# Norm statistics taken by the stages ahead of two norms, and the first of these norms moved into the feed-forward stage, in a six-block decoder on one Trainium2 core

## What is computed

```
x = _layernorm(x + _L0_attn_ref(x, ...))
x = _layernorm(x + _L0_xattn_ref(ctx_2048, ctx_2048, x, ssm_kernel, D, 8))   # a long convolution
x = _layernorm(x + _L0_ffn_ref(x, weight, norm_weight))                      # a quantised linear layer
x = _layernorm(x + _L1_attn_ref(x, ...))                                     # the gated delta rule
x = _layernorm(x + _L1_xattn_ref(x, ctx_2048, ctx_2048, decay))
x = _layernorm(x + _L1_ffn_ref(x, W1, W2))

_layernorm(x): (x - mean) / sqrt(var + 1e-5), mean and var over the 512 features of a token

_L0_ffn_ref(x): xn = x / sqrt(mean(x * x) + 1e-6) * norm_weight
                scale = max(max(|xn|) over all tokens and features, 1e-5)
                xq = round(clip(xn / scale * 127)) / 127 * scale
                out = (xq @ ternary(weight).T) * w_scale
```

## Time and profile before

| | |
|---|---|
| device time, median of 3 runs | 3282.03 us (3278.84 to 3283.53) |
| the profiled execution: its own time, its span | 3278.3 us, 3276.6 us |
| busy over the span: PE, DVE, ACT, POOL | 2951.4, 2576.6, 2401.8, 1950.9 us |
| mean granted TensorE clock | 0.961 of full speed |

### The profile page before, as it was taken

One profiled execution on the slowest core, in us unless ns is written; L12 is line 12 of the kernel. 1 busy time (PEld: TensorE's weight loads), 2 busy tenths in 40 slices (PEclk: granted clock), 3 DMA queues, 4 the chain that ended last, 5 costly groups with the idle time before them and its releaser, 6 DMA issues. The chain is left out here.

```text
span 3276.6 us, 80440 instructions
## 1 busy us (share of the span) xinstructions
PE 2951.4 (90%) x29987; PEld 2015.7 (62%) x30006; DVE 2576.6 (79%) x4692; ACT 2401.8 (73%) x6066; POOL 1950.9 (60%) x2266
## 2 busy tenths in 40 slices
PE   7999887736899999999999999999999999997386
PEld 5666555514566666666676666766766667665243
DVE  4555568885788888888888888888888888886796
ACT  4444343435888888888888888888888888886554
POOL 1111166504877777788777787787877878774000
PEclk9999998968999999999999999999999999999699
DMA  5110043401010110101101011010110101100201
GB/s 219 40 33 27 20 146 108 139 10 58 21 34 21 47 34 23 38 21 47 34 21 40 21 46 34 21 41 21 40 41 21 41 21 36 45 21 1 103 1 52
DMA packets 63473, 146.50 MB, mean 45 GB/s; under 512 B 8704, under 2 KB 17536, under 8 KB 59904
## 3 DMA queue, kind: packets, MB, share of 16 engines
q1 hardware_dynamic: 63104, 141.53, 13.8%
HBM read 128.06 MB, written 13.45 MB: 43 GB/s over the span
## 5 line engine op out<-in xcount | busy, mean ns | idle before, releaser
L2153 DVE TENSOR_TENSOR delta_Pb<-delta_bank,delta_lev 128x512 f16<-128x512 f32 x448 | 310.4, 693 | 148.6 <-PE delta_bank L2482 148.6
L2145 DVE SCALAR_TENSOR_TENSOR delta_F<-delta_bank,delta_cw,delta_F 128x510 f32<-128x510 f32 (+1 forms) x512 | 381.5, 745 | 42.8 <-ACT delta_far L1955 28.7
L2456 PE MATMUL delta_bank<-delta_xh,delta_qkvh 128*128 128x512 f16 x1024 | 390.1, 381 | 6.9 <-DVE delta_F L2145 4.5
L2456 PE MATMUL delta_bank<-delta_xl,delta_qkvh 128*128 128x512 f16 x1024 | 389.2, 380 | 0.0
L2456 PE MATMUL delta_bank<-delta_xh,delta_qkvl 128*128 128x512 f16 x1024 | 388.7, 380 | 0.0
L1695 POOL TENSOR_TENSOR delta_F<-delta_F,delta_far 128x506 f32<-128x506 f32 x256 | 278.4, 1088 | 93.4 <-DVE delta_F L2145 93.4
L1675 POOL TENSOR_SCALAR_AFFINE_SELECT delta_LA<-delta_LA 128x512 f32<-128x512 f32 x128 | 81.5, 637 | 376.3 <-DVE delta_LA L2183 355.4
L2170 DVE CAST delta_XT<-delta_bank 128x512 f16<-128x512 f32 x384 | 262.8, 684 | 50.4 <-PE delta_bank L2501 47.3
L2441 PE MATMUL delta_bank<-delta_zh,delta_xh 128*128 128x256 f16 x1024 | 279.3, 273 | 0.6 <-ACT delta_gz L1977 0.6
L2441 PE MATMUL delta_bank<-delta_zh,delta_xl 128*128 128x256 f16 x1024 | 279.2, 273 | 0.0
L2441 PE MATMUL delta_bank<-delta_zl,delta_xh 128*128 128x256 f16 x1024 | 278.9, 272 | 0.0
(11 more groups left out here) (375 smaller groups left out, 10171.3 us busy)
## 6 DMA issues: line engine op xcount, KB each, us to landing
delta_Gb<-g_rows SPq DMA_DIRECT2D x64, 512.0 KB, 5.3
conv_wf<-in_W SPq DMA_DIRECT2D x72, 256.0 KB, 3.4
delta_st_qkv<-in_Wqkv SPq DMA_DIRECT2D x17, 1024.0 KB, 8.4
conv_T<-filters SPq DMA_DIRECT2D x32, 256.0 KB, 3.4
delta_st_zo<-in_Wz SPq DMA_DIRECT2D x16, 512.0 KB, 8.1
delta_st_zo<-in_Wout SPq DMA_DIRECT2D x16, 512.0 KB, 6.6
conv_ahead_C<-in_ctx_rev SPq DMA_DIRECT2D x1, 6144.0 KB, 27.7
ternary<-conv_spare SPq DMA_DIRECT2D x36, 128.0 KB, 2.8
```

The source lines that it names most:

```text
L2145: ve.scalar_tensor_tensor(dst, src, cw_tap(i, 3 - lag), dst, ALU.mult, ALU.add)\
L2153: ve.tensor_tensor(left(Pb[:, lvl, :, :], lvl), comp(bank[5], lvl), bc(lev[:, lvl, :].rearrange("p (n s) -> p n s", s=1 << lvl), 1, 8), AL ...
L2456: ins = te.matmul(bk[:, :], ww[:, QKV[job], kc, :], xx[:, kc, tok:tok + 512], start=(m == 0), stop=(m == 11))
```

## The change

1. `conv_stage` gets a tensor `mv` and takes the moments itself, behind its last additions: ScalarE for tiles 0 to 8 (`SUMMED_BY_ACT = 9`), each sum as soon as its tile has been added, then the nine squares; VectorE `bn_stats` and `bn_aggr` for tiles 9 to 15 behind its sixteenth addition. ScalarE's unused output goes to `zT`. The ScalarE table set is loaded here.
2. norm1 is no longer a stage. `ffn0_stage` makes rs, nb and `square` from the moments, ScalarE normalises all sixteen tiles, and VectorE scales tile i as soon as it is normalised.
3. The maximum of tile i-1 stands behind the scaling of tile i.
4. `ffn0_stage` takes the moments for norm2 as in 1: ScalarE sums tile i-5 behind its copy of tile i and takes nine squares behind the last copy; VectorE takes seven tiles behind its last addition. `norm_stage` with `moments` skips its own statistics and its table load.

```diff
+SUMMED_BY_ACT = 9
 conv_stage, ScalarE, behind its loop over heads:
+            nc.scalar.preload_act_table_set("natural_log_exp_and_others")
+            for i in range(SA):
+                act.wait_ge(za.sem, za.at(i + 1))
+                nc.scalar.activation(zT[:, :, i * P:(i + 1) * P], X[:, i, :].rearrange("p (a b) -> p a b", a=KC),
+                                     ACT.Identity, accum_out=sm[:, 0, i:i + 1]).then_inc(summed.sem, 1)
+            act.wait_ge(summed.sem, summed.at(SA))
+            nc.scalar.activation(sm[:, 1, :], sm[:, 0, :], ACT.Copy, scale=-1.0 / D).then_inc(squared.sem, 1)
+            act.wait_ge(squared.sem, squared.at(1))
+            for i in range(SA):
+                nc.scalar.activation(zT[:, :, i * P:(i + 1) * P], X[:, i, :].rearrange("p (a b) -> p a b", a=KC),
+                                     ACT.Square, bias=sm[:, 1, i:i + 1], accum_out=sm[:, 2, i:i + 1])\
+                    .then_inc(squared.sem, 1)
 conv_stage, VectorE, behind its additions:
+            for t in range(SA, NT):
+                dve.wait_ge(za.sem, za.at(t + 1))
+                ve.bn_stats(st[:, t - SA, :], X[:, t, :]).then_inc(stats.sem, 1)
+            for t in range(SA, NT):
+                ve.bn_aggr(mv[:, t, :], st[:, t - SA, :]).then_inc(mom.sem, 1)
+            dve.wait_ge(squared.sem, squared.at(SA + 1))
+            ve.tensor_scalar(mv[:, 0:SA, 0], sm[:, 1, :], -1.0, None, ALU.mult).then_inc(mom.sem, 1)
+            ve.tensor_scalar(mv[:, 0:SA, 1], sm[:, 2, :], 1.0 / D, None, ALU.mult).then_inc(mom.sem, 1)
 ffn0_stage, ScalarE:
-            s_.preload_act_table_set("natural_log_exp_and_others")
+            act.wait_ge(g["var"].sem, g["var"].at(1))
+            s_.activation(tn[:, :], var[:, :], ACT.Ln).then_inc(g["root"].sem, 1)
+            act.wait_ge(g["root"].sem, g["root"].at(1))
+            s_.activation(rs[:, :], tn[:, :], ACT.Exp, scale=-0.5).then_inc(g["root"].sem, 1)
             act.wait_ge(g["v"].sem, g["v"].at(1))
             ...
             s_.activation(r[:, :], t[:, :], ACT.Exp, scale=-0.5).then_inc(g["tab"].sem, 1)
+            act.wait_ge(g["shift"].sem, g["shift"].at(1))
+            for i in range(NT):
+                s_.activation(X[:, i, :], X[:, i, :], ACT.Identity, bias=nb[:, i:i + 1], scale=rs[:, i:i + 1])\
+                    .then_inc(g["normed"].sem, 1)
 ffn0_stage, ScalarE, in the loop over tiles behind the copy of tile i, and behind the loop:
+                if 0 <= i - 5 < SA:
+                    sum_of(i - 5)
+            means()
+            for i in range(SA):
+                squares_of(i)
 ffn0_stage, VectorE (ahead of this: var, the Newton step, nb, square):
-            for i in range(NT):
-                ve.scalar_tensor_tensor(xn[:, i, :], X[:, i, :], r[:, i:i + 1], gam[:, :], ALU.mult, ALU.mult)\
-                    .then_inc(g["xn"].sem, 1)
-            for i in range(NT):
+            def largest(i):
                 dve.wait_ge(g["xn"].sem, g["xn"].at(i + 1))
                 ve.tensor_reduce(mx[:, i:i + 1], xn[:, i, :], AX.X, ALU.max, apply_absolute_value=True)\
                     .then_inc(g["mx"].sem, 1)
+            for i in range(NT):
+                dve.wait_ge(g["normed"].sem, g["normed"].at(i + 1))
+                ve.scalar_tensor_tensor(xn[:, i, :], X[:, i, :], r[:, i:i + 1], gam[:, :], ALU.mult, ALU.mult)\
+                    .then_inc(g["xn"].sem, 1)
+                if i >= 1:
+                    largest(i - 1)
+            largest(NT - 1)
 decoder:
-            norm_stage(nc, X, "norm1", square=square)
-            ffn0_stage(nc, X, consts, ahead, a["gamma"], square)
-        norm_stage(nc, X, "norm2")
+                ffn0_stage(nc, X, consts, ahead, a["gamma"], mv1, mv2)
+            norm_stage(nc, X, "norm2", moments=mv2)
```

More of the change, by code:

```diff
@@ L105, with norm_stage @@
 STATS_BY_ACT = 5
-def norm_stage(nc, X, name, guarded=False, square=None, product=None):
+def norm_stage(nc, X, name, guarded=False, moments=None, product=None):
     with ExitStack() as ctx:
@@ L148, in _ @@
                     ve.tensor_scalar(X[:, i, :], X[:, i, :], iM[:, i:i + 1], None, ALU.mult).then_inc(sca.sem, 1)
-            for i in range(SA, NT):
+            for i in range(SA, NT if moments is None else SA):
                 if guarded:
@@ L152, in _ @@
                 ve.bn_stats(st[:, i, :], X[:, i, :]).then_inc(stats.sem, 1)
[L153 to L160 removed]
+            if moments is None:
+                for i in range(SA, NT):
+                    dve.wait_ge(stats.sem, stats.at(i + 1 - SA))
+                    ve.bn_aggr(mv[:, i, :], st[:, i, :]).then_inc(mom.sem, 1)
+                dve.wait_ge(squares.sem, squares.at(SA + 1))
+                ve.tensor_scalar(mv[:, 0:SA, 0], sm[:, 1, :], -1.0, None, ALU.mult).then_inc(moved.sem, 1)
+                ve.tensor_scalar(mv[:, 0:SA, 1], sm[:, 2, :], 1.0 / D, None, ALU.mult).then_inc(moved.sem, 1)
+                dve.wait_ge(mom.sem, mom.at(NT - SA))
+                dve.wait_ge(moved.sem, moved.at(2))
             if guarded:
@@ L218, in _ @@
                     nc.scalar.activation(X[:, i, :], X[:, i, :], ACT.Copy, scale=iM[:, i:i + 1]).then_inc(sact.sem, 1)
-            for i in range(SA):
+            for i in range(SA if moments is None else 0):
                 if guarded:
@@ L224, in _ @@
                     .then_inc(sums.sem, 1)
-            act.wait_ge(sums.sem, sums.at(SA))
-            nc.scalar.activation(sm[:, 1, :], sm[:, 0, :], ACT.Copy, scale=-1.0 / D).then_inc(squares.sem, 1)
-            act.wait_ge(squares.sem, squares.at(1))
-            for i in range(SA):
+            if moments is None:
+                act.wait_ge(sums.sem, sums.at(SA))
+                nc.scalar.activation(sm[:, 1, :], sm[:, 0, :], ACT.Copy, scale=-1.0 / D).then_inc(squares.sem, 1)
+                act.wait_ge(squares.sem, squares.at(1))
+            for i in range(SA if moments is None else 0):
                 nc.scalar.activation(junk[:, i, :], X[:, i, :], ACT.Square, bias=sm[:, 1, i:i + 1],
@@ L755, in conv_stage @@
         zt, za = counter("zt"), counter("za")
+        SA = SUMMED_BY_ACT
+        st, sm = sb("st", [P, NT - SA, 6]), sb("sums", [P, 3, SA])
+        summed, squared, stats, mom = counter("summed"), counter("squared"), counter("stats"), counter("mom")
         NC_ = len(chunks)
@@ L1040, in ffn0_stage @@
         v, t, r = (sb(n, [P, NT]) for n in ("v", "t", "r"))
+        var, tn, rs, nb, square = (sb(n, [P, NT]) for n in ("var", "tn", "rs", "nb", "square"))
+        SA = SUMMED_BY_ACT
+        st, sm = sb("st", [P, NT - SA, 6]), sb("sums", [P, 3, SA])
         mx = sb("mx", [P, NT])
@@ L1126, in _ @@
                                             ALU.add).then_inc(g["add"].sem, 1)
+            for j in range(SA, NT):
+                dve.wait_ge(g["add"].sem, g["add"].at(j + 1))
+                ve.bn_stats(st[:, j - SA, :], X[:, j, :]).then_inc(g["stats"].sem, 1)
+            for j in range(SA, NT):
+                dve.wait_ge(g["stats"].sem, g["stats"].at(j + 1 - SA))
+                ve.bn_aggr(mv_next[:, j, :], st[:, j - SA, :]).then_inc(g["mom"].sem, 1)
+            dve.wait_ge(g["squared"].sem, g["squared"].at(SA + 1))
+            ve.tensor_scalar(mv_next[:, 0:SA, 0], sm[:, 1, :], -1.0, None, ALU.mult).then_inc(g["mom"].sem, 1)
+            ve.tensor_scalar(mv_next[:, 0:SA, 1], sm[:, 2, :], 1.0 / D, None, ALU.mult).then_inc(g["mom"].sem, 1)
         @block.tensor
```

73 lines of the change are left out of this document (46 added, 27 removed).

## The result

The changed kernel took 3263.52 us (median of 5 runs, 3259.36 to 3268.1) beside 3278.84 us of the kernel before (5 runs, 3277.54 to 3283.53): ratio 0.9948, with a 95% interval of 0.9936 to 0.9961. The medians lie 15.3 us apart; the ratio, which is taken over all runs, makes it some 17 us, with an interval of 13 to 21. So the change saves about 0.5% of the time, which is small but clear of the scatter. The profiled execution took 3259.36 us, the shortest of the five, with a span of 3257.3.

A forecast was written before the change was run, and what follows sets the result against it. Three serial stretches between barriers, 87.07 us, were taken as bounding, VectorE pacing the loop. Gains of 11.0 (first) and 3.4 (third), 14.4 rounded to 14.5, off 3282.03 gave 3267.5 us, range 3262 to 3273.

The forecast's parts named there:

- the last one of the sum: Delta stage: its 2323.24 us at granted clock 0.98 taken over unchanged, PE being cold at its start before and after.
- The rival about this clock: Delta stage: earlier arrival leaves PE's clock low for longer, each us costing half; slower from 42 us more; chance 0.03.
- The 93 us at the lower level: Delta stage: time at PE's lower clock level, taken as 4% of 2323 us from the mean granted clock 0.98.
- The starting point: Whole kernel: the gain was taken off 3282.03 us, the median of the runs of before, giving 3267.5.
- as computed: Whole kernel: the gain comes as summed, 3265.5 to 3269.5 us; chance 0.67.
- a case that had 0.04: Whole kernel: little comes of the change, result "same"; would need 8 us of the gain eaten; chance 0.04.
- The prediction's sign of being wrong: First stretch over 35 us, loop additions over 1.6 us apart, or the delta stage's 2323 us moving by over 3.
- to nb: Second norm's start: with moments ready, epsilon and the following small steps reach nb in 1.5 us, where it took 10.08.
- What was to release the first scaling: Feed-forward's start: ScalarE's first normalised tile, not gamma's transfer, releases it 3.5 us behind the stage's start.
- The rival of late gamma: Feed-forward's start: gamma lands 1.9 us later than the first tile, behind the 512 KB loads; gain 12.6; chance 0.12.
- The alternation: Feed-forward's scalings and maxima in turns: same pace, worth nothing itself; rival of lost overlap, gain 12.0, chance 0.08.
- The loop's cover: Quantising loop: ScalarE's sums fit its 0.92 us wait, loop stays 26.16 us; rival of held-up loop, gain 11.8, chance 0.06.

The follow-up runs named there:

- the second pair: The kernel before and the changed kernel, each once more with no edit: 3274.8 us in one run, and 3261.01 us with ratio 0.9945.
- e10: Kernel before, with one idle ScalarE instruction of about 2.4 us at the second norm's end: 3276.19 us beside 3276.33, ratio 0.9999.
- e2: Changed kernel, but the second norm takes its own statistics and table load again: ratio 0.9966 over 6 runs.
- e3: Changed kernel, but the first norm is a stage of its own again, using the moments from the convolution's stage: ratio 0.9971 over 7 runs.
- e4: Changed kernel without the block of weight loads; weights and scales are loaded at the feed-forward's start, behind gamma: 3264.63 us, ratio 0.9947.
- e6: Changed kernel with the sixteen maxima behind the sixteen scalings again: 3259.64 us, ratio 0.9951.
- e8: Changed kernel with each of ScalarE's nine sums in the quantising loop taken twice, second result unused: 3263.52 us in one run.
- e11: The kernel without the load block, gamma first, with six scalings moved from VectorE to ScalarE and GpSimd: 3258.22 us, ratio 0.9947.
- e1: Changed kernel once more with no edit: 3261.01 us over 5 runs, ratio 0.9945.
- e9: Changed kernel with one idle ScalarE instruction of about 1.1 us at the second norm's end: 3264.4 us, ratio 0.996.
- e7: Changed kernel with ScalarE's nine sums moved from the quantising loop to behind it: 3269.48 us in one run.

## Why the prediction was right in its stretch, and which step failed

**The step that failed is the last one of the sum:** "The delta stage (2323.24 us at granted clock 0.98) is taken over unchanged: PE is cold at its start before and after." PE is at the lower level at the start in both, that is so, but the stage did not stay as it was. The clock rises 4.0 us behind the start before and 5.0 us after. With the early rise a fall follows at 14 us, in the middle of the stage's first dense run of matmuls; with the later one it doesn't. The first part of the delta stage is 2.2 us shorter after the change ("gate 7" 215.1 and 212.9; 214.9 and 212.8 in the second pair), a term that the sum put at nothing. The rival about this clock was thought of as a loss only, from a longer time at the lower level, and here it is a gain.

The price in that rival is also too coarse. Up to "gate 7" the kernel before has the early fall (3.4 us) more and the late rise (1.0 us) less, 2.4 us net, which at half a microsecond each would be 1.2 and not 2.2. And e10, which has 0.4 us less at the lower level there than the changed kernel, comes 1.0 us sooner and not 0.2. Argued from the rows, and not tried apart: the fall meets a stretch in which PE is busy throughout, the late rise one with much work on the others (ScalarE is busy for 7.99 of the 8 us from 6 to 14). The 93 us at the lower level came from the rounded 0.98 of a stretch that is 33.5 us longer than the stage; the stage itself shows 0.99, about half of that.

**The starting point was off too.** The forecast set out from 3282.03, the median of 3 runs. The median of the 5 runs beside the changed kernel was 3278.84, 3.2 us lower, and later ones 3278.82, 3275.86 and 3276.33. Both errors pull the same way. Together they are 5.4 us; the measured 3263.5 lies 4.0 below the forecast of 3267.5, and the rest is within the scatter of medians. It lies in the stated range, but 2 us below what the prediction held as computed (3265.5 to 3269.5). That the range held is owed to the width that it has for sessions and rivals. By the prediction's own measure, which tells 0.2%, the change is faster; by one that tells only 2% it would be the same, a case that had 0.04. In the sum, 14.4 + 2.2 = 16.6 us, against 17 measured with an interval of 13 to 21; the times alone can't tell 14.4 from 16.6, the profiles can. The prediction's sign of being wrong, the delta stage moving by more than 3 us, stands at its limit: 2289.73 to 2286.73. Of these 3.0 us 2.2 are the beginning and 1.6 a long piece of the kernel before, told of below; the stage's last piece gave 0.7 back.

**The stretch was right term by term.** Forecast against measured: tail of the convolution 4.9 and 4.8; boundary 2.47 and 2.54; first scaling 3.5 and 3.8; scalings and maxima 20.3 and 20.2 (671.20 to 691.40); to quantising 1.42 and 1.42; loop 26.16 and 26.30; tail behind the loop 5.15 and 5.0; boundary 1.19 and 1.30; to nb 1.5 and 1.5; tiles and boundary to the delta stage 6.0 and 5.8. Sum of the three stretches: a gain of 14.4 forecast, 14.44 measured. e2 and e3 split it as the parts were costed: 3.5 us of part 4, and 3.9 and 7.0 us of the first stretch.

**What was to release the first scaling** was wrong by name: gamma's transfer, not ScalarE's tile. The rival of late gamma had put 1.9 us on it, for two transfers strictly one behind the other. It was 0.3 to 0.4 us, and e4 shows that the order in the queue isn't its cause.

**The alternation** kept its overlap: an operation of 0.75 us with a wait ahead of the next, of another kind, was followed by it after 0.66. The prediction had set a rule of the Trainium skill's page "VectorE: DVE Perf Modes" against this, and had read into it that a wait holds an operation back. The section "The DRAIN you can't avoid" says that the next operation doesn't start until the pipe is empty, but also that the semaphore costs nothing extra. The section "Two Vector instructions with no wait between them" says that a wait doesn't count when it is decided whether an instruction is held. So the page gave no reason for a loss of 2.5 us, and e6 shows none: it gives 0.25 to 0.5 us to the alternation. **The loop's cover** was right, and e8 shows its limit. The 0.14 us by which the loop grew go with the clock: where it rises 6.2 to 6.9 us into the loop, the loop took 26.15 to 26.17 us, with the sums (e3, e6, e11) and without (before), and where it rises at 7.2 to 7.4, 26.21 to 26.30.

**How the rise is set** is shown in part. In the changed kernel, e1, e6 and e9, whose delta stages start 318.6, 318.8, 319.1 and 320.1 us behind the load of the convolution's filters, the clock rises 323.6 to 323.7 us behind that load in all four: it is tied to something before the delta stage, and the stage slides beneath it. In e2, e7 and e8, which start 321.4 to 323.4 us behind the load, it rises at 327.0 to 327.1, and in e4 and e11 (316.7 and 315.9) at 320.3 to 320.4. The tie isn't exact: the two profiles of the kernel before rise at 337.3 and 336.3 with starts 0.8 us apart. Why a rise at 3.6 to 4.4 us is followed by a fall and one at 4.5 to 5.6 isn't is not settled: in e11 (4.4) the fall still came, in e6 (4.5) it didn't. With a rise at 4.5 to 4.6 us "gate 7" comes another 1 us sooner than with one at 5.0 (211.7 to 211.9 against 212.8 and 212.9).

**The long pieces.** Behind the seventh load of gate rows the delta stage has 57 pieces, each from one such load to the next. Each agrees to 0.35 us across all profiles, except that single ones are 1.5 to 1.6 us longer: five of them in e4, two in e3 and e7, one in the first profile of before and in e1, none in the eight others. All eleven are among the pieces in which VectorE makes two `delta_zl` (an operation with two tensor operands in SBUF), one piece in four. In every long piece the first of the two took 2.54 to 2.67 us; in all other pieces of all profiles the first took 0.75 to 0.89, and neither more than 1.65. The same piece in the changed kernel and in e1, where it is long (VectorE's row holds the two together):

```profile
1362.21 2.32 DVE L2169 SCALAR_TENSOR_TENSOR delta_zl<-delta_st_zo,delta_zh 128x512 f16<-128x512 f32 x2
1362.38 1.61 POOL L1834 TENSOR_TENSOR delta_Bl<-delta_LA,delta_Bh 128x512 f16<-128x512 f32 x1
1361.42 4.11 DVE L2169 SCALAR_TENSOR_TENSOR delta_zl<-delta_st_zo,delta_zh 128x512 f16<-128x512 f32 x2
1361.59 1.18 POOL L1834 TENSOR_TENSOR delta_Bl<-delta_LA,delta_Bh 128x512 f16<-128x512 f32 x1
```

Both engines have an operation of two tensor operands in SBUF here, 0.17 us apart. In the first pair GpSimd's is the one that is held up (1.61 us in place of 1.18) and VectorE's is not; in the second GpSimd's keeps its 1.18 and VectorE's takes 2.54. It is the same meeting as that which lengthened the scalings of e11. Up to this point the two profiles agree to 0.02 us, so it turns on hundredths of a microsecond which of the two engines pays. All this is read from the rows and was not tried by an edit. The five are most of why e4's delta stage took 2296.1.

## What to carry to other kernels

In a serial stretch between barriers, sum the chain from durations and start-to-start distances in the trace; that gave each term to a few tenths. Then look at what runs behind the stretch: where a stage starts with PE at the lower level, the moment of its rise against the stage's start can be worth 2 to 3 us, in either direction, and an idle instruction of one or two microseconds ahead of the stage tells whether it is so. And where VectorE and GpSimd both read two operands in SBUF, look for single instructions that are much longer than their kind before calling a difference scatter. Before taking credit for 1 or 2 us of gain in such a stretch, compare the early part of the stage behind it.
